# Pass 1 of a gated-linear-attention block on one core: TensorE's loop written out, and the quarter products placed behind the whole of g, in step 1 ahead of it

## What is computed

```python
h = layernorm(x) * (1 + ca) + sa                      # x: [8192, 512]
q, k, v = h @ Wq.T, h @ Wk.T, h @ Wv.T                # each [8192, 1024], 16 heads of 64
decay = exp(-softplus(h @ Wd.T + bd))                 # one per token and head
k = k * sigmoid(h @ Wg.T)
# per head:  s_t = decay_t * s_(t-1) + k_t^T v_t ;  o_t = q_t s_t
x = x + ga * ((rmsnorm(o) * norm_w * sigmoid(h @ Wog.T)) @ Wo.T)
h = layernorm(x) * (1 + cb) + sb
x = x + gb * ffn(h)
```

## Time and profile before

| | us |
|---|---|
| median of three timed runs (3317.82 to 3320.95) | 3319.93 |
| the profiled execution | 3317.58 |
| its span | 3315.6 |
| TensorE's matmuls (PE) busy | 3225.4, 97% |
| VectorE (DVE) busy | 1887.3, 57% |
| ScalarE (ACT) busy | 1297.9, 39% |
| GpSimd (POOL) busy | 464.8, 14% |
| mean granted clock of TensorE, of full speed | 0.991 |

### The profile page before, as it was taken

The page is one execution under the profiler, slowest core; times in us unless marked ns, Lnnn a source line. Parts: engine busy times, 40 slices in busy tenths (PEclk is TensorE's granted clock), DMA queues, the critical chain, the costliest instruction groups (busy, mean ns, idle before and its releaser), DMA issues. The chain is left out here.

```text
span 3315.6 us, 99291 instructions
## 1 busy us (share of the span) xinstructions
PE 3225.4 (97%) x37253; PEld 2979.0 (90%) x37253; DVE 1887.3 (57%) x4825; ACT 1297.9 (39%) x3584; POOL 464.8 (14%) x723
## 2 busy tenths in 40 slices
PE   7999999999999999999999987999999999999998
PEld 6999899899999999999999977889998999988887
DVE  5455444444454444445444446677667766667776
ACT  3444444444444444444444443333333333333332
POOL 0111111111011111110111112111111111111110
PEclk8999999999999999999999998999999999999999
DMA  6222222222222223222232234222222222233220
GB/s 210 68 97 68 88 85 70 96 72 77 94 67 96 77 68 99 71 76 96 66 98 75 70 128 129 78 76 76 76 76 76 81 84 76 78 89 85 77 76 26
DMA packets 273353, 279.30 MB, mean 84 GB/s; under 512 B 24720, under 2 KB 221344, under 8 KB 273072
## 3 DMA queue, kind: packets, MB, share of 16 engines
q1 hardware_dynamic: 270960, 270.67, 26.7%
q10 hardware_dynamic: 2112, 4.19, 0.4%
HBM read 189.84 MB, written 84.93 MB: 83 GB/s over the span
## 5 line engine op out<-in xcount | busy, mean ns | idle before, releaser
L938 DVE SCALAR_TENSOR_TENSOR mid<-state,w_all,psB 128x64 f32<-128x64 f32 x256 | 71.6, 280 | 517.9 <-PE psB L654 446.2
L55 PE MATMUL psJ<-h_hi,w_g_hi 128*128 128x256 f32 x1024 | 294.8, 288 | 17.1 <-DVE h_lo L842 10.5
L55 PE MATMUL psJ<-h_hi,w_q_hi 128*128 128x256 f32 x1024 | 307.9, 301 | 2.7 <-DVE kg L850 2.7
L55 PE MATMUL psJ<-h_hi,w_k_hi 128*128 128x256 f32 x1024 | 307.3, 300 | 0.7 <-ACT w_new L746 0.7
L55 PE MATMUL psG<-h_hi,w_og_hi 128*128 128x256 f32 x1024 | 287.9, 281 | 9.3 <-PEq L347 5.1
L56 PE MATMUL psJ<-h_lo,w_q_hi 128*128 128x256 f32 x1024 | 285.7, 279 | 0.0
L57 PE MATMUL psJ<-h_hi,w_k_lo 128*128 128x256 f32 x1024 | 285.7, 279 | 0.0
L56 PE MATMUL psJ<-h_lo,w_g_hi 128*128 128x256 f32 x1024 | 285.7, 279 | 0.0
L57 PE MATMUL psJ<-h_hi,w_g_lo 128*128 128x256 f32 x1024 | 285.5, 279 | 0.0
L56 PE MATMUL psJ<-h_lo,w_k_hi 128*128 128x256 f32 x1024 | 285.3, 279 | 0.0
L57 PE MATMUL psJ<-h_hi,w_q_lo 128*128 128x256 f32 x1024 | 284.9, 278 | 0.0
(11 more groups left out here) (238 smaller groups left out, 9403.9 us busy)
## 6 DMA issues: line engine op xcount, KB each, us to landing
cum_rows<-cum_dram SPq DMA_DIRECT2D x512, 64.0 KB, 2.8
grown<-cum_dram SPq DMA_DIRECT2D x256, 128.0 KB
o_dram<-o SPq DMA_DIRECT2D x256, 128.0 KB, 3.1
o_cols<-o_dram SPq DMA_DIRECT2D x128, 256.0 KB, 5.0
an_norm_x<-in_L_attn_x_dram SPq DMA_DIRECT2D x32, 512.0 KB, 6.2
h_dram<-h_hi SPq DMA_DIRECT2D x32, 512.0 KB, 2.8
h_dram<-h_lo SPq DMA_DIRECT2D x32, 512.0 KB, 4.7
h_hi<-h_dram SPq DMA_DIRECT2D x32, 512.0 KB, 4.0
```

The lines of the kernel that those rows point to most:

```text
L55: nc.tensor.matmul(out, w_hi, x_hi, start=first, stop=False)
L938: nc.vector.scalar_tensor_tensor(out=into, in0=mid[:, p % 2, m - 1, :] if m else state[:, p, :], scalar=w_all[:, c, b, p:p + 1], in1=psK[: ...
```

## The change

TensorE's loop over tiles 2 to 29 is replaced by twenty-eight tiles in a row, with constants in the waits. `ready()` is no longer called inside g before its fourth triple but behind g. In step 1 of a tile with a recurrence, `ready()` and the quarter products come first, and g behind them. The other engines' code is the same.

```diff
                 if p == 0 and gla:
                     project(j, "v", 4, pe, ready=ready)
-                elif proj and p > 0:
-                    project(i, "g", p - 1, pe, ready=ready if gla else None)
+                elif proj and p > 0 and not (gla and p == 1):
+                    project(i, "g", p - 1, pe)
+                    if gla:
+                        ready()
                 elif gla:
                     ready()
...
                 elif behind and not proj:
                     turn_k(pe, *behind)
+                if p == 1 and proj and gla:
+                    project(i, "g", 0, pe)
                 if p > 0 and proj:
                     project(i, "q", p - 1, pe)
...
-            with pe.Fori(0, (NT - 4) // 4) as i:
-                for n in range(4):
-                    pe_tile(pe, 4 * i + 2 + n, True, True, 2)
+            for i in range(2, NT - 2):
+                pe_tile(pe, i, True, True, 2)
```

## The result

| | before | after |
|---|---|---|
| median of four timed runs, us | 3320.44 | 3270.35 |
| lowest to highest, us | 3317.82 to 3324.89 | 3268.83 to 3274.77 |
| the profiled execution, us | 3317.58 | 3274.77 |
| its span, us | 3315.6 | 3272.7 |
| TensorE (PE) busy | 97% | 98% |

The ratio is 0.985 (95% interval 0.9833 to 0.9867): 50 us less. The forecast was 3270 us, in a range from 3262 to 3282.

The account below looks back on a forecast made before the run. The prediction took TensorE's queue, busy 97%, to bound pass 1. From the profiled 3317.6 us it took 16.7 (loop written out) and 31.6 (step 1 with constants), giving 3269.3; forecast median 3270 us, range 3262 to 3282.

Parts of the forecast that it names:

- What bounds it: Pass 1 is TensorE's queue, busy 97%; time comes off only where that queue stands still or runs slower.
- Part 1: TensorE's loop over tiles written out: six jumps removed, gaps and lower clock behind two of them included, 16.7 us less.
- The constants: Constants replace computed wait values in the loop: g in step 1 from 2.04 to 1.58 us, 0.46 us per tile.
- Longer code: Each tile's products written once make TensorE's program longer; instruction fetching was taken to cost 0.
- Part 2: Step 1, quarter products ahead of g: transposes to k 4.89 us, 30.2 us less over thirty stretches; 31.6 with tile 31.
- Tile 31: Step 1 without transposes, to q's end: 5.69 us now, 4.25 us then, 1.4 us less.
- first rival: In step 1 q waits for ScalarE's copy of v, 0.3 us everywhere: 9 us come back, 3279 us; 9%.
- the margin: In step 1 of one looped tile, ScalarE's copy of v ends 0.35 us before q would start.
- Part 3: From step 2 on, ready() behind all of g instead of before its last quarter: 0 us, nothing to gain.
- The slower rival: Eight waits directly before the quarter products empty the queue: 110 us, 3379 us; decides from 0.26 us a place; 2%.
- The sum: 3317.6 (profiled execution) - 16.7 - 31.6 = 3269.3 us; 3270 us forecast for the median.

## Why the prediction was right, and where not

**What bounds it.** TensorE's queue: no other engine's wait appeared in tiles 2 to 29 when 50 us were taken from it. That step held.

**Part 1, the gaps.** All six went, with the lower clock behind two of them, and nothing appeared in their place. The prediction says only that a jump costs this; what it is, the wait for the piece of code at the target, came out of the experiments. The size, 16.7 us, was right for the loop of before. It isn't a constant of the loop: with step 1 changed and the loop kept, the same six jumps cost 7 us more. The parts don't add: alone they shorten the inner stretch by 26.4 and 22.0 us, 48.4 in sum, together by 44.4. The constants' 8.2 us are in both, the jumps' 7 us work the other way, which gives 47.2; the last 3 us have no cause of their own, and the spacings of the last section differ by as much between kernels. The forecast avoided this because it counted the loop first and step 1 once. Longer code cost nothing, as forecast: 241 pieces were fetched instead of 261. "Advanced Engine Details and Errata" of the Trainium skill, Control Flow Timing, gives a compare-and-branch about 108 ns, which would have left all this at an estimated 0.65 us; six gaps of 2 to 2.5 us, and 2.7 us for each added jump, disagree with it. Only the branch that leaves the loop, 0.08 us, is near it.

**Part 2, step 1.** The forecast was 30.2 us over thirty stretches, and 28.8 was measured. Term by term for the row above: transposes and changeover 0.96 us as forecast; quarter products 813.39 to 814.49, 1.10 against 1.09; g 1.46 against 1.48; q 1.36 against 1.36. What was mis-sized is that I took one tile for all: about half of the tiles take 4.99 us, since their products stand 0.118 us apart and not 0.113. **The constants**, 0.46 us a tile in the prediction, are 0.3 when tried alone. That didn't spoil the sum, because the new stretch was built from rows of its own and the 0.46 was never added.

**Tile 31** was forecast at 1.4 us and gave 0.8. TensorE and ScalarE there:

```profile
1866.65 0.36 PE L55 MATMUL psJ<-h_hi,w_g_hi 128*128 128x256 f32 x1
...
1868.61 0.38 PE L55 MATMUL psJ<-h_hi,w_q_hi 128*128 128x256 f32 x1 [0.34 <-ACT v L719]
```

```profile
1867.98 0.57 ACT L719 COPY v<-psJ 128x512 f32<-128x512 f32 x1
```

Without the transposes ahead of the quarter products g starts earlier against ScalarE, and q stands 0.34 us for the copy of v. This is the **first rival**, with its mechanism, in the one tile in which the margin was smaller; I had used the margin of a looped tile for it. In the tile shown above the margin is 0.34 us, forecast 0.35.

**Part 3.** 0 was right, by both ways it was tried: with the place put back nothing changed, and with twice the waits nothing was lost. The reason given, that the queue is full there, is borne out. The prediction also said that nothing can be gained, which holds only while kw isn't late.

**The slower rival.** It had the waits themselves empty the queue in the new place. They don't, not even sixteen of them. What costs is a late producer, and in the old place: with kw and qg 1 us later the place inside g costs 0.28 us in the mean, where I had worked out that the gain is used up from 0.26. That kernel is slower than before by 0.3%, 10 us, of which v's 8 us have another cause; so g's share, 51.9 us, alone about uses up the gain of 50, and the point was right. In the new place the same delay costs g nothing. A delay over 1.5 us, from which the new place would wait too, wasn't tried.

**The sum** was 3270, measured 3270.35. Part of that closeness is luck. The terms give 3269.3 for the profiled execution, which lay 2.4 us below the median, so they forecast 3271.7 for the median and not 3270. The sizes were off as well: the inner stretch fell by 44.4 us where the terms gave 46.3, part 1's 16.7 and 29 of the thirty stretches (1.4 of the missing 1.9 in step 1), other stretches differ by up to 1.3 us either way, and the two sets of runs scatter by 6 and 7 us.

## What to carry to other kernels

On an engine whose queue is the bound, put the work whose inputs are ready ahead of the work whose inputs are being made, and build the new stretch from rows of each piece in its new neighbourhood; then look for the next release that has become close, and check it in the tiles at the ends, too. A loop on TensorE here costs 2 to 3 us at each jump, sometimes with a lower clock behind it, depending on where the code lies: write it out when the body is long, and if a loop must stay, try its target some instructions further on. Moving a wait behind more work is worth nothing while its producers are early and a great deal as soon as they aren't, so measure it with the producer made late.

## What the runs showed of the hardware that I had not expected

- **A jump waits for code, and only sixteen products cover it.** At each jump back the sequencer was that far ahead, whatever the products were, and the branch took 3.3 to 4.9 us. The next product started 1.53 to 1.69 us after a 16,384-byte piece of code had landed, and gaps of 1.6 to 3.25 us were seen. "TensorE: Matmul & The Clock Gate" of the Trainium skill gives the engine's queue as 64 deep in its opening table; sixteen products with their weight loads are 32 instructions. What holds the other half isn't settled.
- **Eighteen instructions decided 22 us**, by the second stop (26.1 us of gaps against 11.8) and by the lower clock behind all six jumps or none.
- **The lower clock is hard to foresee.** After gaps of 2.4 to 3.2 us at the same place, in the same kernel, it came four times in six, and with thirteen jumps six times. Among the thirteen it came after a gap of 2.18 us and not after one of 2.92. It cost 1.7 us where twelve products of v ran at half rate, as before. The length of the gap alone doesn't decide it.
- **Products of 256 columns stand 0.113 or 0.118 us apart** for whole stretches at full clock: from q to k in step 1 of after it is 1.36 us for twelve at 815.95 to 817.31, and 1.41 in every other tile. In after the tile lengths repeat every four tiles (58.29, 58.69, 58.56, 58.42 us); in the other two written-out kernels with step 1 changed and no delay added they vary between the same bounds without that pattern. The kernel with ready() twice has an inner stretch 2.9 us shorter than after's (1693.20 against 1696.06), although it only adds waits, so something like this may be the difference. I suppose that it hangs on where the code lies against the fetched pieces; that wasn't tried.
